# Vision transformer on one core: the third split of the up weights, and three more up tiles ahead of the last feed-forward layer

## The reference, cut to what matters

```python
def _L1_ffn_ref(x, w1, w2, w_mfc, w_proj):      # K = 768, hidden width 3072
    pooled = x.mean(axis=1)
    ck = jax.nn.relu(pooled @ w1.T) @ w2.T
    mask = _topk_mask(ck, K)                    # softmax, then 1 at the K largest of each image
    h = jnp.einsum('btd,fd->btf', x, w_mfc) * mask[:, None, :]
    h = jax.nn.relu(h)
    out = jnp.einsum('btf,ef->bte', h, w_proj)
    return out
```

## Time and profile before

| | us |
|---|---|
| median of 3 runs | 1286.76 |
| lowest and highest | 1285.77, 1292.08 |
| the profiled execution | 1287.15 |
| its span on the core | 1285.3 |
| TensorE busy | 1169.0 (91%) |
| VectorE busy | 938.7 (73%) |
| ScalarE busy | 861.5 (67%) |
| GpSimd busy | 457.3 (36%) |

### The profile page before, as it was taken

The page is one execution under the profiler, slowest core; times in us unless marked ns, Lnnn a source line. Parts: engine busy times, 40 slices in busy tenths (PEclk is TensorE's granted clock), DMA queues, the critical chain, the costliest instruction groups (busy, mean ns, idle before and its releaser), DMA issues.

```text
span 1285.3 us, 26614 instructions
## 1 busy us (share of the span) xinstructions
PE 1169.0 (91%) x8874; PEld 1004.8 (78%) x8874; DVE 938.7 (73%) x2392; ACT 861.5 (67%) x3155; POOL 457.3 (36%) x477
## 2 busy tenths in 40 slices
PE   6998879895899999999779999999986898999998
PEld 3995657675788888888568888888874776999998
DVE  5668988984889988988447888888764888444433
ACT  2667778883788888887558888888865543444322
POOL 0001111202434333443043344444414401888754
PEclk9999999997999999999889999999987999999999
DMA  9302002000000000000030000000003442334100
GB/s 371 137 2 75 1 2 75 2 1 1 2 1 2 2 2 2 2 2 1 1 77 2 2 2 2 2 1 2 1 2 107 152 180 81 111 114 122 49 11 16
DMA packets 24595, 55.18 MB, mean 43 GB/s; under 512 B 3982, under 2 KB 21118, under 8 KB 23166
## 3 DMA queue, kind: packets, MB, share of 16 engines
q1 hardware_dynamic: 24460, 53.47, 12.5%
HBM read 39.31 MB, written 14.16 MB: 42 GB/s over the span
## 4 chain that ended last, share of the span: by engine, by line
PE 43%; DVE 19%; ACT 10%; issue 4%; POOL 1%; DVEq 0%; POOLq 0%; ACTq 0%
PE bank L1472 7%; ACT t_p L1212 4%; DVE f_eq L1863 4%; PE bank L1437 4%; DVE t_p L772 3%; PE bank L1416 3%; PE bank L1446 2%; DVE t_raw L748 2%; PE bank L1972 2%; PE bank L1968 2%; PE bank L1973 2%; PE bank L1970 2%; PE bank L1969 2%; PE bank L1396 2%; DVE t_nmax L755 2%
## 5 line engine op out<-in xcount | busy, mean ns | idle before, releaser
L1212 ACT ACTIVATE t_p<-bank,t_nmax 108x108 f32<-108x108 f32 x792 | 270.3, 369 | 35.0 <-DVE t_nmax L755 34.8
L1058 POOL TENSOR_TENSOR t_sq<-t_raw 108x768 f32<-108x768 f32 x88 | 155.4, 1766 | 136.3 <-ACT t_raw L1162 135.9
L2097 POOL TENSOR_TENSOR f_hid_lo<-f_hid,f_hid_hi 128x432 fp32r<-128x432 f32 (+2 forms) x144 | 143.5, 1015 | 107.3 <-ACT f_hid_hi L2083 106.9
L1212 ACT ACTIVATION_READ_ACCUMULATOR t_p<-bank,t_nmax 108x1 f32 x792 | 177.7, 224 | 0.0
L755 DVE TENSOR_REDUCE t_nmax<-bank 108x2 f32<-108x216 f32 (+1 forms) x242 | 122.1, 519 | 52.3 <-PE bank L1437 34.9
L772 DVE TENSOR_TENSOR t_p<-t_p,t_rinv 108x432 f32<-108x432 f32 x198 | 154.9, 782 | 6.8
L2083 ACT CAST f_hid_hi<-f_hid 128x432 fp32r<-128x432 f32 (+2 forms) x144 | 72.4, 515 | 116.3 <-DVE f_hid L2054 96.0
L1220 ACT COPY t_pT<-bank 108x432 f32<-108x432 f32 x198 | 106.8, 541 | 34.9 <-PE bank L1446 34.8
L1446 PE MATMUL bank<-ident,t_p 108*108 108x108 f32 x792 | 109.1, 261 | 22.8 <-ACT t_pT L1220 21.3
L1446 PEld LDWEIGHTS bank<-ident,t_p 108*108 108x108 f32 x792 | 81.4, 133 | 55.2 <-ACT t_pT L1220 36.0
L2054 DVE SCALAR_TENSOR_TENSOR f_hid<-bank,f_maskT 128x432 f32<-128x432 f32 (+2 forms) x80 | 41.5, 518 | 98.9 <-PE bank L1929 97.1
(11 more groups left out here) (228 smaller groups left out, 3329.7 us busy)
## 6 DMA issues: line engine op xcount, KB each, us to landing
spilled<-f_slot SPq DMA_DIRECT2D x56, 216.0 KB, 1.9
f_slot<-spilled SPq DMA_DIRECT2D x56, 216.0 KB, 2.6
A_x<-in_x SPq DMA_DIRECT2D x5, 1728.0 KB, 18.7
A_w<-in_tok_w SPq DMA_DIRECT2D x5, 768.0 KB, 7.5
f_raw_down<-in_w_proj SPq DMA_DIRECT2D x1, 2304.0 KB, 10.7
out_tokens<-h SPq DMA_DIRECT2D x21, 81.0 KB
f_raw<-in_w_mfc SPq DMA_DIRECT2D x3, 512.0 KB, 4.8
f_raw<-in_w_mfc SPq DMA_DIRECT2D x6, 256.0 KB, 6.2
```

What stands on the lines that cost most here:

```text
L1058: pool.tensor_tensor(sq, v, v, ALU.mult).then_inc(s["sq"], 1)
L1212: act.activation(b.p[g % 2][:, m, :], self.scores_of(g, m), ACT.Exp, bias=b.nmax[:, m:m + 1], accum_out=b.rsum[:, m:m + 1]).then_inc(s["ex ...
L2097: pool.tensor_tensor(self.hid_lo[m % 4][:, c], self.hid[m % 4][:, c], self.hid_hi[m % 4][:, c].bitcast(F32), ALU.subtract).then_inc(s["lo" ...
```

## The change

Four edits. Tile t = 12 of units 1, 2 and 3 is added to the spilled tiles: 67 in all, of which 59 are stored and brought back. TensorE's order is written anew: one early tile ahead of the second sum across partitions, two after it, two in each pass, two between the last pass and the third sum, two after that. GpSimd splits the last third only after `pre` 4, when VectorE has scaled its exponentials.

```diff
-        self.spilled = [m for m, (u, g0, n, t) in enumerate(self.order) if u < self.EARLY_UNITS and t % 3]
+        self.spilled = [m for m, (u, g0, n, t) in enumerate(self.order) if u < self.EARLY_UNITS and (t % 3 or u and t == HT // 2)]
...
+        early(0)
         pe.wait_ge(s["pre"], 2)
         across(1, sm[:, 14:15], start=True, stop=True).then_inc(s["across"], 1)
-        early(0)
         early(1)
+        early(2)
         pe.wait_ge(s["padding"], 2)
         for n in range(self.BITS):
             pe.wait_ge(s["count"], n + 1)
             pe.matmul(self.bank[7][:, 0:1], self.both[:, :], self.count[:, 0:1], start=True, stop=True)\
               .then_inc(s["total"], 1)
-            early(2 * n + 2)
             early(2 * n + 3)
+            early(2 * n + 4)
+        early(2 * self.BITS + 3)
+        early(2 * self.BITS + 4)
         pe.wait_ge(s["eq"], 2)
         across(1, sm[:, 17:18], start=True, stop=False)
         across(2, sm[:, 18:19], start=False, stop=True).then_inc(s["across"], 1)
-        for j in range(2 * self.BITS + 2, len(self.early)):
+        for j in range(2 * self.BITS + 5, len(self.early)):
             early(j)
...
         for n in range(3):
             cols = slice(n * HID // 3, (n + 1) * HID // 3)
+            if n == 2:
+
+                pool.wait_ge(s["pre"], 4)
             for m in range(2):
                 pool.wait_ge(s["high"], 2 * n + m + 1)
                 pool.tensor_tensor(self.wu[2 * m + 1][:, cols], self.raw[n][m][:, :],
```

## The result

The changed kernel takes 1282.52 us in the median of 22 runs (1280.70 to 1289.80), the kernel before 1287.19 us in as many. The ratio is 0.9969, with a 95% interval of 0.9955 to 0.9983: some 4.0 us, within 0.5%. The interval does not reach 1.

A forecast was written before the change was run, and what follows sets the result against it. VectorE's chain was taken to bound the selection and TensorE the last layer. Terms -2.2 + 0.1 + 0.8 - 2.9 = -4.2 us gave 1282.6 us against the median of 1286.76, range 1280.4 to 1286.0.

The forecast's parts named there:

- The likeliest case: Whole kernel: the forecast itself, all five parts as taken, -4.2 us to 1282.6 us; chance 0.62.
- The low end of the range: Whole kernel: 1280.4 us, from all good-side bounds at 1281.6 and a fastest run 1.0 under the median.
- Part 1: Ahead of the loop: with GpSimd's split waiting, VectorE's scaling L1857 takes 0.95 us, not 3.13; gain 2.18 us.
- Part 2: One early tile ahead of the second sum costs 0; first pass loses 0.1 us, bounds 0 and 1.4.
- Part 3: In the loop: each pass still issues two tiles and two stores and stays 2.49 us; cost 0.
- Part 4: Behind the loop: two tiles fill the gap at no cost; a clock fall at the mask loses 0.8 us, bounds 0 to 1.7.
- Part 5: Last layer: three up tiles fewer on a TensorE that never waits, gain 2.9 us, bounds 0 to 2.95.
- No fall: Rival at the mask: TensorE's clock does not fall there; 1281.8 us, chance 0.17.
- GpSimd as the bound: Rival in the last layer: GpSimd bounds it where five slot tiles come in a row; 1285.5 us, chance 0.05.
- a lasting fall: Rival at the last layer's start: the clock's fall at the mask lasts; 1289.3 us for 15 us, chance 0.04.
- L1857 not held: Rival ahead of the loop: GpSimd did not hold L1857, or the wait moves on to L1858; 1284.8 us, chance 0.08.

The follow-up runs named there:

- the wait alone: The kernel before with only GpSimd's new wait (`pre` 4) ahead of splitting the last third; ratio 0.9981 to the kernel before.
- the quarters: The kernel before, without the new wait, each of the last third's two GpSimd splits cut into four; 300.76 us from TensorE's first logit matmul to the end.
- the kernel without the wait: The changed kernel with GpSimd's new wait taken out again; ratio 0.9977 to the kernel before.
- The filler's kernel: The changed kernel with 11 matmuls of no use where TensorE waits for the mask; ratio 0.9963 to the kernel before.

## Why the prediction was right, step by step

The sum was -4.2 us and 1282.6 us. The ratio gives -4.0 (with the interval, -2.2 to -5.8), the median is 1282.52; the traces of the stage give -3.4 to -3.8. The likeliest case came about, with one term under its true size. That the median was met within 0.1 us is luck: the stage gained 0.4 to 0.8 us less than the sum, and the median of the kernel before moved from 1286.76 to 1287.19 with more runs. The low end of the range is 0.2 us off its own sum too: 1281.6 less 1.0 is 1280.6, not 1280.4; nothing hangs on it.

- **Part 1, the wait: right.** -2.18 was forecast and -2.11 measured, in the changed kernel and in the wait alone. With GpSimd idle the scaling takes 1.02 us, the value from the rows at other widths rather than the 0.88 of the subtraction. The two splits lay beside the first two counts at no cost (counts of 1811 to 1815 ns), and the small copy (L1865 now) was not held, with 0.15 us. That the hold ends with GpSimd's instruction was an inference from one trace; the quarters show it.
- **Part 2: right in kind.** The tile ahead of the second sum cost nothing. The first pass lost 0.24 us in the first trace and nothing in the two later ones, where the clock rose 0.7 us sooner; 0.1 was taken. The argument that TensorE, longer at work, would bring the rise forward is not borne out: with early(0) ahead of the sum it rose at +15.1, as before, or at +14.4, as it also did in the quarters, which have the old order. Tiles at 1.2 GHz within the loop did come up once, in the kernel without the wait, in its second and third pass and not in the first, for which the bound was given.
- **Part 3: right.** The passes behind the first take 2.49 us, as before.
- **Part 4: the effect came, but its reason was wrong, and it was undersized.** A loss of 0.8 us was forecast for a fall at the mask; it came in all three traces of the changed kernel and cost 1.5 to 1.6, near the upper bound of 1.7. "The gap of 2.02 us brought a fall, the pair 0.94 and 1.41 none; 2.6 is beyond both" doesn't hold: 2.5 us brought none in three traces of two other kernels, and 0.56 and 0.95 were each followed by one. So far as it rested on that reason, the forecast of a fall was lucky. Nor did the fall stretch the way from the mask to the down tiles: in the two later traces the transposes took 1.7 us, not 1.53, but TensorE then idled 1.25 us and not 1.41, so that from the transposes' start to the first down tile it is 2.94 us in the trace of before and in all three of after. The two tiles behind the loop cost nothing, as forecast, and the third sum stayed on time.
- **Part 5: right.** -2.91 forecast; 197.5 - 194.6 = 2.9 to 3.0 in traces without a fall. No wait for GpSimd came in at such places, whether three or five of them.
- **The rivals.** No fall, GpSimd as the bound, a lasting fall, L1857 not held: each was looked for and not found in the changed kernel. The filler's kernel shows what no fall would have been worth: a stage of 296.3 us.

What decides the fall is **open**. It depends on more than the length of the idle time ahead of it. Where a kernel was traced two or three times, the clock fell behind the mask each time or never, which speaks against plain chance by execution; but only four kernels were traced more than once, and the late and the early rise are a second thing that no run held fixed. The gap behind the transposes is left open in twelve traces, from eight kernels, and seven of them had no fall. So the two traces with no fall in which both gaps are filled would show little by themselves; that each filler can be set against its own kernel at the same rise makes it likely that the filling is why, and does not show it. What makes the rise late or early wasn't looked into.

## What to carry to other kernels

A tensor_scalar of VectorE from SBUF to SBUF, without accumulator, can be held until the end of the GpSimd tensor_tensor that runs; the count over the same columns, with its accumulator, was not (3.13 us against 1.02, and 1.81 in either case). One wait on GpSimd's side, which had some 7 us to spare, brought VectorE's chain 2.1 us forward; cutting GpSimd's instruction into quarters brought it 1.6 forward without any wait. Where one stage leaves TensorE idle and the next is bound by it, each tile moved is worth its full time (0.97 us here), but look at the granted clock behind the new gap, where more than such a tile can be lost. And when single executions spread by 9 us for reasons ahead of the change, measure from a mark at the start of the changed stage: that brought differences of 0.1 us into sight. Then compare only traces in which the clock rose at the same place.

## What was not expected of the hardware

The granted clock has a say in the order of 1 us in a stage like this, and the same stage takes different courses: low stretches of 3.4 or 6.8 us, in the loop, behind it, or in the first down tiles, with the same gaps around them. The kernel before showed both lengths at nearly the same place in two executions. The gap of 2.0 us behind the loop was followed by a fall in four of the six traces that have it, and the one of 2.5 us ahead of the transposes was followed by a fall in three of six.
